# Attention products of four heads: one block over 512 queries instead of two halves at two places of a loop round

## What is computed

```python
scores = jnp.einsum("bnhd,bmhd->bhnm", q, k) * scale
scores = jnp.where(mask, jnp.float32(-jnp.inf), scores)
attn = jax.nn.softmax(scores, axis=-1)
h = jnp.einsum("bhnm,bmhd->bnhd", attn, v).reshape(b, n, d)
h = h @ Wo + bo
```

## Time and profile before

| | |
|---|---|
| time, median of 3 runs | 1221.51 us (1218.25 to 1221.82) |
| profiled execution | 1220.38 us, span 1218.7 us |
| granted TensorE clock, mean | 0.989 |
| PE busy | 1167.3 us, 96% |
| DVE busy | 985.6 us, 81% |
| ACT busy | 923.9 us, 76% |
| POOL busy | 483.1 us, 40% |
| probabilities times values (L876), PE | 125.2 us, 2048 records |
| chain that ended last | PE 89%, DVE 4%, ACT 3% |

### The profile page before, as it was taken

The page is one execution under the profiler, slowest core; times in us unless marked ns, Lnnn a source line. Parts: engine busy times, 40 slices in busy tenths (PEclk is TensorE's granted clock), DMA queues, the critical chain, the costliest instruction groups (busy, mean ns, idle before and its releaser), DMA issues.

```text
span 1218.7 us, 28047 instructions
## 1 busy us (share of the span) xinstructions
PE 1167.3 (96%) x9452; PEld 853.8 (70%) x9452; DVE 985.6 (81%) x2680; ACT 923.9 (76%) x2112; POOL 483.1 (40%) x337
## 2 busy tenths in 40 slices
PE   5977999999999999999999999999999999999896
PEld 2854677777777777777777777777777777777563
DVE  4675788888888988888898888889888888987776
ACT  3234887888878788887878888787888878788684
POOL 1352233453363335336333533633353363334320
PEclk9799999999999999999999999999999999999999
DMA  8115152432615244261524326152432615222311
GB/s 241 36 35 143 31 166 43 122 88 60 166 37 162 48 122 88 66 160 37 162 47 122 87 64 163 36 163 46 122 88 65 162 36 155 55 70 70 104 37 36
DMA packets 170686, 114.03 MB, mean 94 GB/s; under 512 B 107185, under 2 KB 152241, under 8 KB 170545
## 3 DMA queue, kind: packets, MB, share of 16 engines
q1 hardware_dynamic: 168384, 104.37, 33.2%
q0 software_dynamic: 2160, 7.87, 1.9%
HBM read 61.87 MB, written 25.17 MB: 71 GB/s over the span
## 4 chain that ended last, share of the span: by engine, by line
PE 89%; DVE 4%; ACT 3%; issue 2%; DMA 1%; POOL 0%; DVEq 0%; ACTq 0%; SPq 0%; POOLq 0%
PE ps_j L759 36%; PE ps_t L772 22%; PE ps_j L876 9%; PE ps_s L751 8%; PE ps_s L745 7%; PE ps_j L893 4%; ACT probs L927 2%; PE ps_j L884 1%; DVE masked_s L1023 1%; PE ps_j L843 1%; DVE y_l L1173 1%; ACT pt_h L933 0%; PE ps_j L783 0%; DMA xt<-xs 0%; DMA xt<-ys 0%
## 5 line engine op out<-in xcount | busy, mean ns | idle before, releaser
L1023 DVE CUSTOM_DVE_ANT_0 masked_s<-ps_s,mask 128x512 f32<-128x512 f32 x640 | 424.3, 680 | 19.0 <-PE ps_s L751 17.1
L927 ACT ACTIVATE probs<-masked_s,nm_h 128x512 f32<-128x512 f32 x512 | 367.2, 718 | 83.1 <-DVE nm_h L1023 76.8
L772 PE MATMUL ps_t<-ident,probs 128*128 128x128 f32 x2560 | 390.8, 276 | 11.9 <-ACT pt_h L933 6.4
L772 PEld LDWEIGHTS ps_t<-ident,probs 128*128 128x128 f32 x2560 | 305.9, 142 | 96.8 <-issue 27.8
L933 ACT ACTIVATE pt_h<-ps_t 128x512 f32<-128x512 f32 x404 | 237.8, 589 | 71.2 <-PE ps_t L772 68.5
L751 PE MATMUL ps_s<-stack 128*128 128x512 f16 x512 | 194.4, 380 | 2.2 <-DVE nm_h L1023 2.1
L759 PE MATMUL ps_j<-xw,pt_l 128*128 128x256 f16 x1536 | 189.2, 274 | 0.0
L759 PEld LDWEIGHTS ps_j<-xw,pt_l 128*128 128x128 f16 x1536 | 151.3, 99 | 30.7
L600 POOL TENSOR_TENSOR rstd_L<-var_eps_L,minus_half 128x4 f32<-128x4 f32 x32 | 32.8, 1024 | 295.5 <-DVE var_eps_L L1053 295.5
L876 PE MATMUL ps_j<-pt_h,v 128*32 128x256 f32 x2048 | 125.2, 386 | 2.2 <-DVE pt_h L1030 1.9
L1058 DVE TENSOR_TENSOR pt_l<-ps_t,pt_l 128x512 f16<-128x512 f32 x128 | 88.3, 690 | 43.2 <-ACT pt_l L933 29.0
(11 more groups left out here) (116 smaller groups left out, 1609.5 us busy)
## 6 DMA issues: line engine op xcount, KB each, us to landing
stack<-bounce SPq DMA_DIRECT2D x256, 128.0 KB, 3.1
bounce<-parts SPq DMA_DIRECT2D x64, 256.0 KB, 2.7
adj_t<-adj_dram SPq DMA_DIRECT2D x30, 512.0 KB, 5.3
x<-x_dram SPq DMA_DIRECT2D x16, 512.0 KB, 3.9
out_dram<-y_f POOLq DMA_DIRECT2D x15, 512.0 KB, 3.4
stack<-adj_dram SPq DMA_DIRECT2D x2, 512.0 KB, 5.9
pt_h<-l_wc SPq DMA_DIRECT2D x2, 256.0 KB, 4.1
xt<-ys SPq DMA_TRANSPOSE x32, 4.4
```

Of the source, the lines that this page charges most:

```text
L772: last = pe.transpose(ps_t[r % 2][:, t], probs[:, r, t * P:(t + 1) * P], ident[:])
L927: act.activation(probs[:, r], masked_s[:, r], ACT.Exp, bias=nm[:, n, r:r + 1], scale=-1.0, accum_out=total[:, n, r:r + 1]).then_inc(exps, 1)
L1023: dve.tensor_tensor_reduce(out=masked_s[:, r], in0=ps_s[scores_bank(pos)][:], in1=m[:, r], scale=-scale, scalar=NONE_LEFT, op0=ALU.add, op ...
```

## The change

The table places `OG` of the first four heads at tile 5 instead of 3 and 5, and that of the last four at 23 instead of 22 and 24, in each of the fourteen rounds; the transposes of the reciprocals stay at 7 and 26. In the tail three blocks go from 3, 4 to 4, from 19, 21 to 20 and from 35, 37 to 37, and the last one of these has its reciprocals at 39 instead of 40. The very last block of all keeps its two halves under a new name, `OE`. A block is 16 matmuls of 512 columns where there were 32 of 256, and waits for all four copies of the last head. Semaphore counts follow.

```diff
-    ("OG", (1, 0), "i", 0, (3, 5, 7)),
+    ("OG", (1, 0), "i", 0, (5, 7)),
...
-    ("OG", (1, 2), "i", 1, (22, 24, 26)),
+    ("OG", (1, 2), "i", 1, (23, 26)),
...
-    ("OG", (2, 0), "i", 0, (3, 4, 6)),
+    ("OG", (2, 0), "i", 0, (4, 6)),
...
-PARTS = {"AV": 4, "OG": 3, "R": 1, "N": 1, "S": 1, "B": 1, "C": 1, "D": 1, "M": 1}
+PARTS = {"AV": 4, "OG": 2, "OE": 3, "R": 1, "N": 1, "S": 1, "B": 1, "C": 1, "D": 1, "M": 1}
...
+        def products_done(b, g):
+
+            return 2 * b + g + (2 if (b, g) == (NB - 1, 1) else 1)
+
...
-                if name == "OG":
+                if name in ("OG", "OE"):
                     g, r = l, half
-                    if r < 2:
-
-                        for tile in range(2 * r, 2 * r + 2):
+                    pieces = 1 if name == "OG" else 2
+                    if r < pieces:
+
+                        tiles = range(NT // pieces * r, NT // pieces * (r + 1))
+                        at = slice(tiles[0] * P, (tiles[-1] + 1) * P)
+                        for tile in tiles:
                             pe.wait_ge(*copied(blk_.slot_of("H", 4 * g + 3, b), tile))
...
-                                last = pe.matmul(out_bank[h * HD:(h + 1) * HD, 2 * r * P:2 * (r + 1) * P],
-                                                 v1[:, b % 2, t, col:col + HD], pt_of(b, 4 * g + h)[:, t, 2 * r * P:2 * (r + 1) * P],
+                                last = pe.matmul(out_bank[h * HD:(h + 1) * HD, at],
+                                                 v1[:, b % 2, t, col:col + HD], pt_of(b, 4 * g + h)[:, t, at],
...
-                    dve.wait_ge(done["O"], 2 * (2 * b + g + 1))
+                    dve.wait_ge(done["O"], products_done(b, g))
```

More of the change, by code:

```diff
@@ L90 @@
     ("N", None, "i+1", 1, (1,)),
-    ("OG", (2, 0), "i", 0, (3, 4, 6)),
+    ("OG", (2, 0), "i", 0, (4, 6)),
     ("QH", (1, 2), "i+1", 0, (7, 8)),
     ("QH", (0, 1), "i+1", 1, (10, 11)),
-    ("OG", (0, 1), "i", 1, (19, 21, 24)),
+    ("OG", (0, 1), "i", 1, (20, 24)),
     ("R", None, "i", 1, (19,)),
@@ L98 @@
     ("R", None, "i+1", 0, (34,)),
-    ("OG", (2, 0), "i+1", 0, (35, 37, 40)),
+    ("OG", (2, 0), "i+1", 0, (37, 39)),
     ("R", None, "i+1", 1, (51,)),
-    ("OG", (1, 2), "i+1", 1, (51, 51, 51)),
+    ("OE", (1, 2), "i+1", 1, (51, 51, 51)),
     ("WO", (0, 1), "i+1", 0, (51, 51)),
@@ L396, in occupy @@
                     return before
-                side = half // 2 if name in ("AV", "OG") else half
+                side = half // 2 if name in ("AV", "OE") else half
                 before = self.in_bank.get(banks[side], ())
@@ L981, in job @@
                         .then_inc(hi_ready["QK"[half]], 1)
-                if name == "OG" and half == 2:
+                if (name, half) in (("OG", 1), ("OE", 2)):
                     g = l
```

## The result

The changed kernel took 1279.46 us (median of 4 runs, 1278.19 to 1279.83) against 1219.88 (median of 4, 1217.36 to 1221.82) in the same comparison: ratio 1.0486, 95% interval 1.0465 to 1.0508. The profiled execution took 1279.56 us with a span of 1277.7.

A forecast was written before the change was run, and what follows sets the result against it. PE (TensorE), busy nearly the whole loop, was taken as the bound. 1220.4 us + 32.9 for waits at both places over 14 rounds + 18.6 for the clock + 1.9 for the tail = 1274 us, range 1250 to 1282.

The forecast's parts named there:

- the mechanism: Loop, second place: PE waits for ACT's copy of tile 23, then the clock drops; this case was given 0.66.
- The block takes 3.57 us and the merge saves 0.30: Each of 31 merges: one 512-column block costs 3.72 us with entry and exit, against 4.02 for two halves.
- First place +0.1 us per round: Tile 5: the 0.30 saved is eaten by a wait of some 0.4 us for the copy of tile 2.
- Second place, the wait for the copy of tile 23, 2.25 us per round: Tile 23: PE idles for ACT's copy; 2.25 us lost per round, the merge's 0.30 already inside.
- The clock, 11.2 drops of 1.66 us = 18.6: Behind the loop's 14 waits: half clock after 11.2 of them, each 1.66 us, between 0 and 23.2 us in all.
- The share of 4 in 5: Part of the 14 loop waits expected to bring half clock, from four of five earlier idle stretches.
- The reason given for the price: A drop was said to cost its full 1.66 us because PE is what all wait for.
- The list of idle stretches: Five PE idle stretches over 1.8 us in the earlier trace; half clock after four, none after the first, 2.90 us.
- The tail +1.9: After the loop: 1.7 us at the first place, bound by DVE's copy of tile 3, and 0.1 at each other.
- The third place: Last merged block of the tail, its head copied in time: +0.1 us, between -0.3 and +0.5.
- The saving is lost, nothing gives it back: Behind the second place, up to T27 (tile 27's transposes): PE is full again, so the 2.25 us stays lost.

The follow-up runs named there:

- the pair with the filler: Changed kernel with eight throwaway fp16 matmuls in the second place's idle stretch: 1259.46 us; the same with the copies waited for last: 1255.77 us.

## Why the prediction was right, step by step

The time lies 5 us above the forecast 1274, inside the range of 1250 to 1282, and the mechanism is the one that was forecast. Part of the closeness is luck: a round with a drop was forecast 2.35 + 1.66 = 4.01 us longer and measured 75.09 - 71.07 = 4.02, but with a wait that was 0.23 too small and a drop that was 0.22 too dear.

- *The block takes 3.57 us and the merge saves 0.30*: measured 3.57 in the changed kernel, and 6.92 against 7.23 us from T3 to T6 where no wait eats it.
- *First place +0.1 us per round*: 0.10 in the rounds of the run with it alone, 1.6 us in its time.
- *Second place, the wait for the copy of tile 23, 2.25 us per round*: T23 0.80 after T22 as worked out (0.79), and the copy's end at 3.70 (3.69). But both places together cost 2.58 and not 2.35. The mis-sized part is the 0.15 us from the end of the copy to the block: it is 0.36, 699.74 to 700.10. It had been read where the block's second half waits for copies only the earlier trace rows; the merged block has two more waits behind the copies, for the values and for the bank, fulfilled long ago, and steps through them first. With these in front, 0.21 us are gone. 14 x 0.23 = 3.2 us of the 5.
- *The clock, 11.2 drops of 1.66 us = 18.6*: there were fourteen drops, and each cost 75.09 - 73.65 = 1.44. 14 x 1.44 = 20.2. The share of 4 in 5 was too low, the price too high, because the half clock began 0.45 us before the block, inside the wait: 3.41 - 0.45 = 2.96 us, half of it 1.48. In the first rounds, where the half clock began only with the block, a drop cost up to 1.7. The reason given for the price, that all others wait for PE, holds in the loop; at the place in the tail from which the 1.66 was read, the drop was free, as the run with the first place shows. The list of idle stretches on which the share rested was short by one, 11.88 us at the very start of the kernel, and the one without a drop was the longest but this, so the count says little about what a stretch of 2.25 us does. All fourteen gaps of 2.4 us had half clock with them. The Trainium skill, "TensorE: Matmul & The Clock Gate", section "Why this matters for your kernels", by whose advice gaps of this length would pass, is not borne out here.
- *The tail +1.9*: in the changed kernel about 3.5, in the run with the tail alone 2.0 to 2.4. The third place was mis-sized: it had 0.1 us and costs 0.8 to 0.9. The second costs 0.4. The first had 1.7 and costs 1.4 in the run with the tail alone and 2.2 in the changed kernel. The difference there is how the half clock of 6.83 us stands to the block. In the run with the tail alone it reaches 1140.53 - 1136.96 = 3.57 us into the block; in the changed kernel, below, 1198.00 - 1192.81 = 5.19 us, half of the difference being 0.8 us.

```profile
1192.81 6.19 PE L883 MATMUL ps_j<-pt_h,v 128*32 128x512 f32 x32 [3.01 <-DVE pt_h L1037]
```

```profile
1191.17:1198.00 6.83, 5.19 (x28) 0.50 0.31 27
```

- *The saving is lost, nothing gives it back*: T24 to T27 is 707.67 - 705.11 = 2.56 us, as worked out (2.57), and the round behind it has its old length.

The sum from the measured terms: 14 x 2.58 + 14 x 1.44 + 3.5 = 59.8 us, and the span grew by 59.0. Against the forecast the wait is 3.2 us more, the clock 1.6 and the tail 1.6.

## What to carry to other kernels

On an engine that is never idle, a job cut in two is not only overhead: its first half is what the engine does while the last input of the second half is being made. Before merging, ask which input comes last and what will stand in front of the wait; here the merge was worth 0.3 us, and a round lost 2.6 with that already taken off. An idle stretch on TensorE can have a second price, the clock; where the wait can't be removed, throwaway matmuls inside it can keep that price down (three of them brought back 20 us of 59 here). And put the wait that ends last behind the others.

## What was not expected

The length of a round locks to the drops of the clock. In the changed kernel, in the one with the second place alone and in the one with the copies waited for last, the rounds are 75.09 to 75.11 us, though undisturbed they would differ by 0.1 and 0.2 us. The block's start in two rounds of the changed kernel, the first row with half of its records:

```profile
625.02 3.36 PE L883 MATMUL ps_j<-pt_h,v 128*32 128x512 f32 x16 [2.43 <-ACT pt_h L940]
...
775.18 5.09 PE L883 MATMUL ps_j<-pt_h,v 128*32 128x512 f32 x32 [2.43 <-ACT pt_h L940]
```

The drops come 75.09 us apart (699.65, 774.74), and they do so from the first round on, when the rounds do not yet. The first four drops start at 174.00, 249.09, 324.18 and 399.28, the first four blocks at 173.74, 249.11, 324.50 and 399.97, which is 75.37, 75.39 and 75.47 us apart. The first two drops as windows:

```profile
174.00:177.41 3.41, 3.41 (x20) 0.50 1.03 262
249.09:252.50 3.41, 3.39 (x17) 0.50 1.10 275
```

A drop that starts earlier against the block lies more in the wait and costs less, so a round that would be late is shortened and one that would be early is lengthened: the start of the half clock against the block settled at -0.45 us in the changed kernel and at +0.02 in the one with the reordered waits, which paid back its 0.21 us to the clock. That this is what holds the length fast is a reading that fits these rounds; no run set the time of the drops by itself. The run with the reordered waits is weak evidence for it, since it comes to this length without any pull: a round without a drop is 73.42 us, a drop wholly inside the block costs 5.34 - 3.64 = 1.70, together 75.12. With two matmuls of filler it did not settle: the rounds with a drop were 75.3 us, and twice one passed without a drop. The consequence is practical. While drops of the clock come in every round, a real improvement of a few tenths per round can be hidden in the time. It shows when the drops are taken away, as in the pair with the filler.
